# A latent-attention layer on one core: the output projection done as seven block products for each pair of heads

## The reference

```
h = layernorm(x)
q = rmsnorm(h @ wq_a.T) @ wq_b.T           # 16 heads, 128 plain + 64 rotary columns each
kv_c, k_pe = split(h @ wkv_a.T)            # 128 latent columns, 64 rotary
k_nope, v = rmsnorm(kv_c) @ wkv_b.T        # 16 heads, 128 + 128
attn = softmax(q k / sqrt(192))            # 512 x 512 per head
x = x + concat_heads(attn @ v) @ wo.T      # the output projection
x = x + ffn(layernorm(x))                  # 512 -> 1536 -> 512, gated, fp8-rounded weights
```

## Time and profile before

| | |
|---|---|
| median of three timed runs | 2230.62 us |
| span of the profiled execution, first to last instruction | 2228.8 us |
| TensorE clock granted, mean | 0.999 of 2.4 GHz |
| matmuls in the trace | 10977 |
| chain that ended last | PE 93%, DVE 3%, ACT 1%, DMA 1%, POOL 1%, issue 1% |
| exponentials, float32 and float16 (L1077, L1079) | 512 each, 698 and 700 ns |
| additions of the projection (L1449) | 508 with rden, 743 ns |
| time of DMA packets | 47.7% of 16 engines |

### The profile page before, as it was taken

One profiled execution on the slowest core, in us unless ns is written; L12 is line 12 of the kernel. 1 busy time (PEld: TensorE's weight loads), 2 busy tenths in 40 slices (PEclk: granted clock), 3 DMA queues, 4 the chain that ended last, 5 costly groups with the idle time before them and its releaser, 6 DMA issues.

```text
span 2228.8 us, 34908 instructions
## 1 busy us (share of the span) xinstructions
PE 2205.4 (99%) x10977; PEld 1026.8 (46%) x10977; DVE 1557.8 (70%) x3227; ACT 1066.6 (48%) x2345; POOL 1001.5 (45%) x688
## 2 busy tenths in 40 slices
PE   7999999999999999999999999999999999999999
PEld 5444544445444454444544445444454445444454
DVE  7888887776477764777648775587755877467773
ACT  6667564554255542555325553355443554345532
POOL 4657465453355524454244642536334363343322
PEclk9999999999999999999999999999999999999999
DMA  7868336562175631756216561365614564145530
GB/s 248 188 124 150 88 71 142 106 124 51 23 151 105 122 53 34 145 105 127 44 43 146 106 121 29 73 123 106 118 25 104 106 115 95 24 104 109 106 65 19
DMA packets 703800, 219.42 MB, mean 98 GB/s; under 512 B 685520, under 2 KB 685776, under 8 KB 702672
## 3 DMA queue, kind: packets, MB, share of 16 engines
q1 hardware_dynamic: 703696, 218.09, 47.7%
HBM read 40.78 MB, written 8.39 MB: 22 GB/s over the span
## 4 chain that ended last, share of the span: by engine, by line
PE 93%; DVE 3%; ACT 1%; DMA 1%; POOL 1%; issue 1%; SPq 0%; DVEq 0%; POOLq 0%
PE bank L853 13%; PE bank L291 11%; PE bank L293 11%; PE bank L292 11%; PE scores L863 7%; PE scores L663 5%; PE scores L293 5%; PE scores L291 5%; PE scores L292 5%; PE bank L674 4%; PE bank L675 4%; PE bank L676 4%; PE scores L660 3%; PE bank L840 1%; PE bank L689 1%; PE scores L557 1%
## 5 line engine op out<-in xcount | busy, mean ns | idle before, releaser
L1716 POOL TENSOR_TENSOR arena<-arena 128x1024 f16<-128x1024 f32 x256 | 545.7, 2132 | 620.3 <-ACT arena L1079 620.3
L1077 ACT ACTIVATE arena<-scores,shift 128x512 f32<-128x512 f32 x512 | 357.5, 698 | 535.0 <-DVE shift L1429 494.8
L1449 DVE SCALAR_TENSOR_TENSOR arena<-bank,rden,arena 128x512 f32<-128x512 f32 x508 | 347.9, 743 | 137.0 <-PE bank L293 137.0
L1427 DVE TENSOR_REDUCE mx<-scores 128x1 f32<-128x512 f32 x512 | 352.5, 689 | 20.5 <-PE scores L293 16.7
L1079 ACT ACTIVATE arena<-scores,shift 128x512 f16<-128x512 f32 x512 | 358.6, 700 | 0.0
L853 PE MATMUL bank<-arena,WFF 128*128 128x512 f16 x1392 | 313.5, 379 | 0.8 <-DVE arena L1601 0.6
L1774 POOL TENSOR_TENSOR arena<-arena 128x512 f16<-128x512 f32 x96 | 114.4, 1191 | 255.6 <-ACT arena L1152 255.6
L853 PEld LDWEIGHTS bank<-arena,WFF 128*128 128x128 f16 x1392 | 135.9, 98 | 164.1 <-DVE arena L1601 2.3
L291 PE MATMUL bank<-WVO,arena 128*128 (+1 forms) x512 | 194.2, 379 | 2.4 <-DVE arena L1222 1.2
L1222 DVE SCALAR_TENSOR_TENSOR arena<-bank,arena 128x512 f16<-128x512 f32 (+1 forms) x263 | 176.2, 670 | 29.1 <-ACT arena L1070 24.4
L663 PE MATMUL scores<-arena 128*128 128x512 f16 x512 | 195.4, 382 | 0.0
(11 more groups left out here) (159 smaller groups left out, 3480.5 us busy)
## 6 DMA issues: line engine op xcount, KB each, us to landing
arena<-arena SPq DMA_TRANSPOSE x712, 3.2
arena<-w_ffn SPq DMA_DIRECT2D x24, 384.0 KB, 3.5
arena<-x SPq DMA_DIRECT2D x8, 1024.0 KB, 5.6
out<-arena SPq DMA_DIRECT2D x32, 256.0 KB, 2.0
arena<-x SPq DMA_DIRECT2D x14, 512.0 KB, 4.4
WVO<-w_o SPq DMA_DIRECT2D x4, 1024.0 KB, 8.2
arena<-w_nope SPq DMA_DIRECT2D x4, 768.0 KB, 9.1
arena<-down_scale SPq DMA_DIRECT2D x8, 256.0 KB, 3.3
```

Source lines behind the costliest of these rows:

```text
L1077: act.activation(P32[:, t, :], SC[:, t, :], ACT.Exp, scale=EXP_SCALE, bias=shift[:, t:t + 1], accum_out=esum[:, par, t:t + 1]).then_inc(s[ ...
L1427: dve.tensor_reduce(mx[:, t:t + 1], SC[:, t, :], AX_X, ALU.max).then_inc(s["mxr"], 1)
L1449: dve.scalar_tensor_tensor(out=XR[:, t, :], in0=banks[t][:, :], scalar=by[:, t:t + 1], in1=XR[:, t, :], op0=ALU.mult, op1=ALU.add).then_in ...
L1716: pool.tensor_tensor(PL[:, par, two, :], P32[:, two, :], PH[:, par, two, :], ALU.subtract).then_inc(s["pl"], 1)
```

## The change

In batches 2 to 7 the first fourteen heads are taken as seven pairs (E, O). The projection of a pair is the product of [CT_E CT_O] (512 rows) with the two stacked blocks of WVO. It is cut in 2 x 2 blocks, rows by halves and columns by halves (256 each), and done with seven products of blocks instead of eight, some of them of sums of blocks (a scheme of the Strassen-Winograd kind). Each block product is two tiles of 256 columns by three matmuls: 42 matmuls of 256 columns a pair in place of 24 of 512.

What follows from it:

- Batches 0 and 1 stay plain. In batch 1 POOL (`block_sums`, ten operations of 256 columns a pair, `block_sums_lo`, one of 1024), ACT (`sum_hi`) and SP make the blocks of weights and write them to DRAM (`w_duo`). From batch 2 on the seven blocks of a pair are loaded by SP, four early and three late (`early_blocks`, `late_blocks`), into the memory of WVO's first fourteen heads.
- Since two heads are mixed before the addition, the exponentials are divided by their sum beforehand. ACT (`probs_divided`) makes four float32 exponentials, then for each tile a scaled float16 copy and, for three of the four tiles, a scaled float32 copy in place. POOL multiplies the fourth tile. DVE computes the reciprocals (`reciprocals`) after its maxima, and thus after ACT's exponentials of the same head.
- The values and projection of a head come one step later: at step i PE does scores i, values i-2, absorb i+2, and at even steps from 4 the early products, at odd ones the late products (`duo_step`).
- DVE writes the context in float32 (`context_rows`), ACT its high part (`context_hi`, between the copies of the first tile), DVE its low part (`context_lo`); POOL forms the block sums (`context_sums`, `context_sums_rest`) at odd steps. Eight additions a pair (`add_block`) go into XR, without the reciprocal.
- Heads 14 and 15 stay as they were. The layer norm of the next input moves from POOL to DVE, ACT and POOL, and the order of the last down products changes.

```diff
+N_TWO = 0
+            def duo_product(j, x, w, k, start):
+                for t in range(2):
+                    dst = DBANK[k][:, t * HB:(t + 1) * HB]
+                    for m, (p, q) in enumerate(((0, 0), (0, 1), (1, 0))):
+                        r = pe.matmul(dst, lhsT=XP[j % 2][:, p, x, tile(t)], rhs=WB[:, q, w, :],
...
+            def duo_early(b, j, parts=range(N_EARLY)):
...
+                    if x == X_O1:
+                        pe.wait_ge(s["cth"], b * N_CT + min(2 * j + 3, 2 * N_DUO))
+                        pe.wait_ge(s["ctl"], b * N_CT + min(2 * j + 3, 2 * N_DUO))
...
+            def duo_late(b, j):
+                pe.wait_ge(s["w_late"], 16 * n)
+                pe.wait_ge(s["outr"], base + 4)
...
+            def duo_step(b, i):                                      # PE
+                scores(b, i // 2, i % 2)
+                if i >= 2:
+                    values(b, i // 2 - 1, i % 2)
+                if i >= 4 and i % 2 == 0:
+                    duo_early(b, (i - 4) // 2, (0,))
+                if i == 5:
+                    duo_early(b, 0, (2, 3))
+                absorb(i + 2, b * NH + i + 2)
+                if i >= 4 and i % 2 == 0:
+                    duo_early(b, (i - 4) // 2, (1,) if i == 4 else (1, 2, 3))
+                elif i >= 5:
+                    duo_late(b, (i - 5) // 2)
...
+            def probs_divided(b, i):                                 # ACT
+                for t in range(NT):
+                    act.wait_ge(s["shift"], NT * g + t + 1)
+                    if i > 0 and t % 2 == 0:
+                        act.wait_ge(s["pl"], 2 * g - 1 + t // 2)
+                    act.activation(P32[:, t, :], SC[:, t, :], ACT.Exp, ...)
+                for t in range(NT):
...
+                    if t == NT - 1 or t == NT - 2 and i < N_TWO:
+                        act.wait_ge(s["nm3"], by_pool(b, i, t))
+                        act.activation(PH[:, par, t, :], P32[:, t, :], ACT.Copy)
+                    else:
+                        act.activation(PH[:, par, t, :], P32[:, t, :], ACT.Copy, scale=rden_duo[:, par, t:t + 1])
+                        act.activation(P32[:, t, :], P32[:, t, :], ACT.Copy, scale=rden_duo[:, par, t:t + 1])
+                    if t == 0 and i >= 2:
+                        context_hi(b, i - 2)
...
+            def duo_step(b, i):                                      # DVE
+                maxima(g)
+                reciprocals(b, i)
+                if i >= 2:
+                    context_rows(b, i - 2)
+                if i >= 4 and i % 2 == 0:
+                    duo_adds(b, (i - 4) // 2, (0,))
+                if i == 5:
+                    duo_adds(b, 0, (2, 3))
+                if i >= 2:
+                    context_lo(b, i - 2)
+                if i >= 4 and i % 2 == 0:
+                    duo_adds(b, (i - 4) // 2, (1,) if i == 4 else (1, 2, 3))
+                elif i >= 5:
+                    duo_adds(b, (i - 5) // 2, (4, 5, 6, 7))
+                qa_lo(g + 2, i % 2)
...
+            def head_divided(b, i):                                  # POOL
+                pool.wait_ge(s["rdn"], 2 * n + 2)
+                for t in (NT - 2, NT - 1) if i < N_TWO else (NT - 1,):
+                    pool.tensor_tensor(P32[:, t, :], P32[:, t, :], rden_duo[...].broadcast_to((P, S)), ALU.mult)
+                if i >= 3 and i % 2:
+                    context_sums(b, (i - 3) // 2)
...
```

More of the change, by code:

```diff
@@ L470, in batch @@
                         weight_chunk(c)
+                if not first and not last:
+                    early_blocks(b + 1, 0)
+                    late_blocks(b + 1, 0)
+                    if ahead:
+                        next_input(b + 1)
                 if not last:
@@ L511, in _ @@
             output_matrix(3)
-            batch(0, False, first=True)
-            with sp.Fori(1, B - 1) as b:
+            batch(0, False, first=True, plain=True)
+            batch(1, False, plain=True)
+            with sp.Fori(B_PLAIN, B - 2) as b:
                 batch(b, False)
+            batch(B - 2, False, ahead=False)
             batch(B - 1, True)
@@ L1095, in attention @@
                     act.wait_ge(s["yo"], b * NT)
-                probs(base, 0, True)
+                if not plain:
+                    act.wait_ge(s["t_out"], 16 * N_DUO)
+                if plain:
+                    probs(base, 0, True)
+                else:
+                    probs_divided(b, 0)
                 qa_hi(base + 2, 0)
@@ L1112, in attention @@
                         head_step(i, base, i % 2, chunk=chunk_of(i), weights=True)
[L1113 to L1117 removed]
+                elif plain:
+                    for i in range(2, NH - 2):
+                        head_step(i, base, i % 2)
+                        if i >= 3 and i % 2:
+                            sum_hi((i - 3) // 2)
+                        if 7 <= i < 7 + NT:
+                            next_rows_hi(b, i - 7)
+                else:
+                    for i in range(2, NH - 2):
+                        probs_divided(b, i)
+                        qa_hi(base + i + 2, i % 2)
+                        if i in STG_STEPS and not last:
+                            next_rows_hi(b, STG_STEPS.index(i))
                 for k in range(2):
@@ L1212, in _ @@
             setup_queries_and_keys()
-            batch(0, False, first=True)
-            with act.Fori(1, B - 1) as b:
+            batch(0, False, first=True, plain=True)
+            batch(1, False, plain=True)
+            with act.Fori(B_PLAIN, B - 1) as b:
                 batch(b, False)
@@ L1642, in ffn @@
                                              op1=ALU.mult).then_inc(s["yt"], 1)
-                if last:
-                    for t in range(2, NT):
+                    if last and t >= 2:
                         dve.wait_ge(s["yt"], b * NT + t + 1)
@@ L1746, in attention @@
+            def attention(b, last, first, plain):
                 base = b * NH
@@ L1752, in attention @@
                 for i in range(NH):
-                    head(base + i, i % 2)
-                    if i == 0:
+                    if plain:
+                        head(base + i, i % 2)
+                    elif i < 2 * N_DUO:
+                        head_divided(b, i)
+                    else:
+                        last_heads(b, i)
+                    if plain and not first and i >= 2:
+                        if i % 2 == 0:
+                            block_sums(i // 2 - 1)
+                        else:
+                            block_sums_lo(i // 2 - 1)
+                    if i == 0 and plain:
                         for n in range(N_ROT_FFN + 1, N_ROT):
@@ L1760, in attention @@
                         join_chunk(chunk_of(i - 1))
-                    if 0 <= i - start < NT and not last:
-                        next_norm(b, i - start, stg)
+                    if plain and 0 <= i - start < NT:
+                        if first:
+                            next_norm(b, i - start, stg)
+                        else:
+                            next_rows_lo(b, i - start)
+                    if not plain and not last and i in STG_STEPS:
+                        next_rows_lo(b, STG_STEPS.index(i))
             def ffn(b, last, first):
@@ L1802, in _ @@
             rotate(0, NT)
-            batch(0, False, first=True)
-            with pool.Fori(1, B - 1) as b:
+            batch(0, False, first=True, plain=True)
+            batch(1, False, plain=True)
+            with pool.Fori(B_PLAIN, B - 1) as b:
                 batch(b, False)
```

536 lines of the change are left out of this document (465 added, 71 removed).

## The result

The changed kernel takes 2285.34 us (median of four runs, 2279.19 to 2288.5), against 2230.2 us for the kernel before. The ratio is 1.0241, with a 95% interval of 1.0226 to 1.0256: slower, by 55 us.

What follows compares the result with a forecast made beforehand. PE was taken as the bound, without gaps inside a batch, so any new wait is lost in full. From 2230.6: - 24.9 + 51 + 13 + 2 = 2271.7, said as 2271 us; range over all cases 2212 to 2298.

Steps and rivals of the forecast that it cites:

- Columns: PE's projection of a head pair: 5.18 us before, 4.59 after; 24.9 us gained over 42 pairs if nothing else waits.
- Start of a batch: Steps 0 to 4: PE waits for exponentials and, 4.0 us, at product O1; 8.5 us a batch, 51 in all.
- the loop: DVE maxima, ACT exponentials, copies and qa_hi, DVE qa_lo, next maxima: 9.9 to 10.6 us a head, hidden in mid-batch.
- POOL's hold on P32: After an odd step POOL's low part ends just when the next head's third exponential wants P32: 0 to 0.3 us late.
- End of a batch: Pair 6 and the last projection: DVE's additions bind, the projection waiting 0.7 us; 2.2 us a batch, 13 in all.
- The addition's 1.5: At pair 6 product S3 waits for DVE's fourth addition, ready at 20.2 against 18.7 for PE: 1.5 us.
- issued a step ahead: nothing: Loads of weight blocks, 0.9 MB a pair, cost nothing; without that cover a load would be 4 us late, 42 times.
- rival C: PE's granted clock falls to 1.2 GHz behind a 4 us gap in each of six batches: 12 to 30 us, 2288; chance 0.10.
- Batch 1: POOL's ten weight sums make low parts of odd heads 1 to 3 us late: 0 to 8 us, taken as 2.
- A: The gain is kept, with a shorter loop or no waits at the batch start: 2206, up to 2226; chance 0.24.
- B: The loop also binds in the middle of a batch, at 0.5 us more a head: 2291; chance 0.15.
- D: Waits and gain are equal over the whole kernel: 2226 to 2235; chance 0.04.

Runs made afterwards that it cites:

- v9_sums: v5_order with early context order only at batch start, input norm's DVE part later, POOL's sums ahead of low parts except head 3; 2226.41 us (0.9978).
- v1_qalo: The changed kernel with one DVE instruction moved: the next head's qa_lo behind the maxima instead of before them, heads 2 to 13; 2271.70 us (1.0180).
- v2_pool: v1_qalo with POOL's sums of context blocks put behind both low parts of the exponentials at odd heads; 2268.92 us (1.0179).
- v5_order: v2_pool plus earlier late load, head 15's values split, context_rows between reciprocal halves, context_hi ahead of copies, two XE buffers; 2256.60 us (1.0116).
- e2_noload: The changed kernel without the load of pair 6's three late blocks, that pair being multiplied with pair 5's; 2268.27 us (1.0171).
- e1_fill: The changed kernel with 14 needless 512-column matmuls on PE before product O1 at step 4 of each batch from 2 on; 2272.91 us (1.0200).

## Why the prediction was right

The direction held and the time lay in the range; the move was 55 us where 41 were forecast. That the sum came so near is in part luck: the start of a batch was priced 22 us too high, and the wait for the late load (18 us) and the falls of the clock (17 us) were not in the sum. By its own steps:

- **Columns, -24.9.** Right. The 256-column block products start 0.109 us apart, and v9_sums reaches the forecast batch but for its waits.
- **Start of a batch, 51 us (8.5 a batch).** The mechanism was right: v1_qalo cut the loop with one instruction and gained 14 us. At O1 the loop was not alone: its wait was 3.2 us, 2.98 in v1_qalo, 2.4 to 2.75 in v2_pool, and 1.1 only in v5_order, where the context no longer stands behind all the reciprocals. The prediction had that order in its sum, and POOL's hold on P32 at 0 to 0.3. The waits measured 1.7 + 3.2 = 4.9 a batch, 29 us in all. The term was too large because the loop was: 9.34, 9.69 and 9.83 us a head against 9.9, 10.4 and 10.6. The copies were right (starts 0.613 apart against 0.61). Two latencies were not. Late maxima follow each other in 0.79 us; the 0.86 of the earlier trace rows is PE's pace. And the next maximum starts 0.60 behind a qa_lo, not 0.72. Besides, context_hi starts 5.2 behind the first maximum, right behind the second copy, where 5.7 had been put.
- **End of a batch, 13 us (2.2).** The place was right and the cause named was second in line. The addition's 1.5 measured 1.3 (e2_noload) and the last projection's 0.7 measured 0.6. In front stood 2.5 to 3.7 us for the late load, which hid the addition's. The prediction's step "issued a step ahead: nothing" failed there: it holds in the middle, but at pair 6 SP's queue had the transposes of head 15 in front of it.
- **The clock (rival C, 0.10).** It came true on top of the main case. The prediction put one fall of 2 to 5 us at O1 in each of six batches. There were nine behind twelve long gaps, three at O1 and six at the late load, for about 17 us in all. Had C been a term of the sum and not a rival, that would have been more than the miss of 14.
- **The rest.** Batch 1 cost 3.0 against 2.
- **Rivals A, B and D** fell: no gain was kept, and in the middle steps PE shows no waits.

"TensorE: Matmul & The Clock Gate" of the Trainium skill, section HAM oscillation — how this bites in real kernels, has idle gaps between bursts bring the clock down. By that rule, the trace agrees in kind: 0.61 in the window behind O1's gap in batch 3, and 1.00 in e1_fill, where the gap is filled; but behind the same gap the clock stayed at 1.00 in three batches of six.

What is not settled: which of the long gaps make the clock fall. Its mean differed between runs of the changed kernel (0.990 to 0.994), and the times with it (2288.5 to 2279.2 us).

## What to carry to other kernels

When the bound engine has no idle time, a change that saves its work must be followed through the other engines as a chain in order, head by head, and above all where a pipeline starts and ends, since there the bound engine has least to hide them with. Look for the one instruction that closes a loop between two engines, and for a transfer whose issue stands behind an unrelated wait in its queue: moving one of each gave 14 and 17 us here. Order on two or three engines can be late by nearly the same amount; then each move shows little until the last. Where long gaps on TensorE can't be avoided, price the clock's fall as part of them.

## What the runs showed of the hardware that was not expected

- Filling a 3.2 us gap with 14 needless matmuls made the kernel 12.4 us faster over six batches (e1_fill). About 5 us of that lie at the filled gaps and 7 at other gaps, behind which the clock then fell less often.
- Behind a gap of 3.0 to 3.1 us the granted clock fell in three batches of six and stayed at 1.00 in the others (the changed kernel, O1).
- POOL multiplies 512 float32 by a broadcast column in 1.04 us (L2230), where its difference of two full operands, written as float16, takes 1.19.
- ACT's scaled copy of 512 float32 from SBUF takes 0.711 us whether it writes float16 or float32 in place.
